# Cross-attention of a perceiver block on one core: values as the stationary operand in the attend, the chunk's sum turned back, and part of the next chunk's keys and values moved in PE's order

## The chip, the cores and the metric

The kernel runs on one core of a Trainium2 chip (the chip has eight). The metric is device time in microseconds of one launch, median of the runs shown. The engines are named as the profile names them: PE (TensorE, with PEld for its weight loads), DVE (VectorE), ACT (ScalarE), POOL (GpSimd), SP (SyncE). PE's clock has two levels, 1.2 and 2.4 GHz; the profile shows the granted clock as a share of the higher one.

## The reference, cut to what matters

Three blocks follow each other on x (8 batches of 128 queries, 512 wide): a cross-attention over a context of 2048 keys (384 wide) with a mask, a self-attention, and a quantised MLP. The change lies in the first.

```python
def _L0_xattn_ref(x, context, mask, W_q, W_k, W_v, W_o, b_o):
    HEADS, DIM_HEAD = 8, 64
    q = (x @ W_q).reshape(b, n, HEADS, DIM_HEAD)
    k = (context @ W_k).reshape(b, j, HEADS, DIM_HEAD)
    v = (context @ W_v).reshape(b, j, HEADS, DIM_HEAD)
    sim = jnp.einsum('bihd,bjhd->bhij', q, k) * DIM_HEAD ** (-0.5)
    sim = jnp.where(mask[:, None, None, :], sim, max_neg)
    attn = jax.nn.softmax(sim, axis=-1)
    out = jnp.einsum('bhij,bjhd->bihd', attn, v).reshape(b, n, INNER)
    return out @ W_o + b_o
x = x + _L0_xattn_ref(_layernorm(x), ctx_768, mask, ...)
x = x + _L0_attn_ref(_layernorm(x), ...)
x = x + _L0_ffn_ref(_layernorm(x), ...)
```

## The kernel before

Everything stays on one core, engine programs are written out by hand and meet through semaphores. The cross-attention walks over batches b and, in each, over chunks of 256 keys (NC = 8 for a batch). A chunk whose keys are all masked is skipped: each engine reads the same bits into a register and branches over it (`live`, lines 260 to 264). With this data 13 of 64 chunks are live, one or two in a batch. The softmax is done with a running maximum: each chunk scales the batch's sum `o_all` by `alpha` and adds its own part.

To keep float32 accuracy, keys and values are products of split operands: `hi` is the rounded part, `lo` the rest, and a product is three terms over three slices of the context (`product`, lines 561 to 572): hi by hi, lo by hi, hi by lo, so nine matmuls.

One live chunk n on PE (`chunk`, lines 659 to 721) works for itself and for the next live chunk, `ahead` = n + 1:

- `scores(g)` (663 to 675) makes the scores of heads 2g and 2g+1, three pairs of matmuls, each with 64 rows of the array, into banks 3 and 4. It waits until DVE has taken the maxima of the pair before.
- `turn_context(ahead)` (623 to 634) transposes the next chunk's context: four transposes into bank 0, two into bank 1.
- `keys(ahead, g)` (636 to 649) makes a quarter of the next keys: nine matmuls of 256 columns; keys 0 and 1 into bank 2, keys 2 and 3 into bank 0.
- `turn(g)` (677 to 688) transposes the probabilities of a pair of heads, four transposes into bank 5 or 6.
- `values(ahead, t)` (651 to 657) makes half of the next values: nine matmuls of 512 columns into bank 1 (t = 0) or bank 2 (t = 1).
- `attend(g)` (690 to 701) multiplies the turned probabilities of a pair (the stationary operand, 128x128) with the values (64 moving columns): two heads by two key tiles, which the trace shows as eight matmuls; the result lies queries by (head, dim) in bank 7.

The order is written out in lines 703 to 721:

```python
scores(0); turn_context(ahead); scores(1); keys(ahead, 0); turn(0)
keys(ahead, 1); scores(2); attend(0); turn(1); keys(ahead, 2)
scores(3); attend(1); turn(2); keys(ahead, 3); values(ahead, 0)
attend(2); turn(3); values(ahead, 1); attend(3)
```

ACT (lines 1044 to 1076) takes the exponentials (`exp(h)`, 1047), copies the turned probabilities of even pairs (`prob_copy`, 1052), rounds the next context (`context_high`, 1030) and the next keys (`key_high`, 1036), and copies the next values (`value_copy`, 1040); it casts the context behind the first two exponentials, and copies the values at the end, when the last attend is done. DVE (lines 1441 to 1487) takes the maximum of a head while it scales and biases its scores (`top(h)`, 1444, into `probs` and `negm`), makes the low parts (`context_low`, 1428, `key_low`, 1436; both run in the helper `low`, line 1342), copies the turned probabilities of odd pairs (1453), rescales `l_all` and `o_all`, and adds bank 7 to `o_all` at the chunk's end (1487, `o_done`).

After the live chunks of a batch PE projects the output of the batch before (`project_output`, line 738) and turns this batch's normalised output and the norm of an earlier one (723 to 736), while all engines step over the masked chunks. SP loads the context of the chunk after next once the transposes of the next have read the buffer (line 325).

The self-attention further down (`attend2`, lines 836 to 847) has the values as the stationary operand, 64 columns wide, and writes two heads to the two halves of the partitions.

Of the kernel before, what the change touches and what calls it, by code (L numbers as in the profile page):

```python
# [14 lines left out]
P = 128  # L15
# [10 lines left out]
def bass_perceiver_block_kernel(nc, x, ctx_768, mask, xa_wq, xa_wk, xa_wv, xa_wo, xa_bo,  # L26
# [29 lines left out]
    with ExitStack() as ctx:  # L56
# [42 lines left out]
        p2_odd1 = sb("p2_odd1", [P, 512])  # L99

# [95 lines left out]
        def sems(engine, names):  # L196
# [10 lines left out]
        (xnT_ps, code_ps, qT_ps, cxT_ps, kT_ps, s_ps, v_ps, pT_ps, pv_ps, onT_ps, lnT_ps, xo_ps, v2_ps, mean_ps, qk_ps,  # L207
         s2_ps, pT2_ps, o2_ps, y2_ps, wT_ps, xqT_ps, g_ps, u_ps, hqT_ps, y_ps) = sems(
            "pe", "xnT_ps code_ps qT_ps cxT_ps kT_ps s_ps v_ps pT_ps pv_ps onT_ps lnT_ps xo_ps v2_ps mean_ps qk_ps "
            "s2_ps pT2_ps o2_ps y2_ps wT_ps xqT_ps g_ps u_ps hqT_ps y_ps")  # L210
        (wq_hi, wk_hi, wo_hi, xnT_hi, qTall_done, qT_hi, cxT_hi, kT_hi, v_done, p_done, alpha_done, pT_act, onT_hi, lnT_hi, xo_done,
         wv2_hi, v2_act, wqk_hi, qT2_done, p2_done, pT2_act, tern_rounded, wo2_hi, oT_hi, wT_act,
         xq_done, xqT_done, sg_done, h_round, hq_done, hqT_done, y_scaled) = sems(
            "act", "wq_hi wk_hi wo_hi xnT_hi qTall_done qT_hi cxT_hi kT_hi v_done p_done alpha_done pT_act onT_hi lnT_hi xo_done "
# [342 lines left out]
        def _(pe):  # L557
# [78 lines left out]
            def keys(n, g):  # L636
                if g == 0:
                    pe.wait_ge(v_done, START + CT * n)
                elif g == 2:
                    pe.wait_ge(cxT_lo, START + 2 * n + 1)  # L640

                def waits(a, b, k):
                    if g == 0 and a == "hi" and k != 1:
                        pe.wait_ge(cxT_lo if b == "lo" else cxT_hi, START + 2 * n + k // 2 + 1)

                last = product(key_bank[g // 2][:, (g % 2) * CHUNK:(g % 2 + 1) * CHUNK],
                               lambda k, w: part(wk, w)[:, k, g * P:(g + 1) * P], lambda k, w: part(cxT, w)[:, k, :], CK, waits)
                if g % 2:
                    last.then_inc(kT_ps, 1)

            def values(n, t):
                if t == 0:
                    pe.wait_ge(cxT_lo, START + 2 * n + 2)
                else:
                    pe.wait_ge(kT_lo, START + 2 * n + 1)
                product(value_bank[t][:], lambda k, w: part(cxT, w)[:, k, t * P:(t + 1) * P],
                        lambda k, w: part(wv, w)[:, k, :], CK).then_inc(v_ps, 1)

            def chunk(b, n):
# [17 lines left out]
                def turn(g):  # L677
                    pe.wait_ge(p_done, START + H * n + 2 * g + 2)
                    if g == 0:
                        pe.wait_ge(onT_lo, START + b)  # L680
                    if g == 1:
# [8 lines left out]
                def attend(g):  # L690
                    if g == 0:
                        pe.wait_ge(v_done, START + CT * n + CT)
                        pe.wait_ge(o_done, START + n)
                    pe.wait_ge(pT_dve if g % 2 else pT_act, START + 2 * n + g // 2 + 1)
                    for j in range(2):
                        h = 2 * g + j
                        for t in range(CT):
                            at = (CT * j + t) * P
# [1127 lines left out]
```

## Time and profile before

| what | value |
|---|---|
| runs shown | 780.3, 784.73, 784.78 us, median 784.73 |
| profiled execution | 780.1 us, span 778.4 us |
| mean granted clock of PE | 0.947 |
| live chunks of the cross-attention | about 68 to 391 us of the span |

The span runs from the first to the last instruction; the execution's own time has a little around it. A row of a timeline has the start and the length in us, engine, line of the kernel, operation, output and inputs by their names, array tile or size, and a count; in brackets what the engine waited for and how long. Rows of one line that follow each other are merged into one, whose length reaches from the first start to the last end. Matmuls overlap, so the next group often starts before the last has ended.

### The profile page before, as it was taken

How to read it: one execution, taken by the hardware profiler on the slowest of the kernel's cores; microseconds unless marked ns; L12 is line 12 of the kernel's file. 1: busy time of each engine (PE TensorE's matmuls, PEld its weight loads, DVE VectorE, ACT ScalarE, POOL GpSimd, SP SyncE). 2: the span in 40 equal slices, each digit the busy share in tenths (PEclk: the TensorE clock that was granted, in tenths of full speed). 3: DMA queues.
4: the chain of work that ended last, by engine and by line, in shares of the span. 5: the costliest groups of instructions: out<-in, count | busy, mean ns of one | idle time of the engine just before them, and what ended most of it. 6: DMA issues, size and time to landing. Idle time of an engine off the chain costs nothing.

```text
span 778.4 us, 14709 instructions
## 1 busy us (share of the span) xinstructions
PE 665.1 (85%) x4244; PEld 519.8 (67%) x4244; DVE 442.5 (57%) x960; ACT 356.1 (46%) x846; POOL 109.7 (14%) x143
## 2 busy tenths in 40 slices
PE   2896597969969696978969989999999899889996
PEld 1675486858858585867858867777777678634553
DVE  6822344444545444554475766666666534699974
ACT  2233233424434233433441136666666534468984
POOL 2581000010010101010020002222222100012211
PEclk9998888988989987998989999999999999999999
DMA  8000000000000000000545774444453243000111
GB/s 311 23 22 22 2 21 21 22 2 22 22 20 22 2 21 22 22 2 20 190 167 193 272 274 163 163 163 163 163 163 136 109 163 118 6 1 15 27 25 42
DMA packets 40064, 64.86 MB, mean 83 GB/s; under 512 B 4056, under 2 KB 20440, under 8 KB 40032
## 3 DMA queue, kind: packets, MB, share of 16 engines
q1 hardware_dynamic: 40032, 64.45, 24.3%
q8 instruction: 18, 0.29, 0.2%
q14 instruction: 14, 0.11, 0.0%
HBM read 53.95 MB, written 10.49 MB: 83 GB/s over the span
## 4 chain that ended last, share of the span: by engine, by line
PE 64%; DVE 13%; issue 11%; DMA 4%; DVEq 3%; ACT 2%; POOL 1%; SPq 0%; ACTq 0%; POOLq 0%
PE bank L570 33%; PE bank L699 6%; PE bank L930 5%; PE bank L687 3%; DMA absw<-in_L_ffn_w_down_dram 3%; PE bank L672 3%; PE bank L938 2%; PE bank L845 2%; PE bank L589 2%; DVE asum L1584 2%; DVE tern L1634 2%; DVE xn_a L1353 1%; PE bank L822 1%; PE bank L880 1%; PE bank L833 1%
## 5 line engine op out<-in xcount | busy, mean ns | idle before, releaser
L1049 ACT ACTIVATE probs<-probs,negm 128x256 f32<-128x256 f32 x104 | 52.1, 501 | 109.0 <-DVE negm L1450 109.0
L1450 DVE CUSTOM_DVE_ANT_0 probs<-bank,bias,negm_old 128x256 f32<-128x256 f32 x104 | 46.0, 480 | 64.2 <-PE bank L672 62.1
L672 PE MATMUL bank<-kT_hi,qT_hi 64*128 64x256 f32 x104 | 23.2, 440 | 51.6 <-issue 47.8
L930 PE MATMUL bank<-w_T,xqT 128*128 128x512 bf16 x256 | 58.4, 379 | 4.6 <-ACT xqT L1231 2.0
L467 POOL TENSOR_TENSOR rstd<-var_eps,neg_half 128x1 f32 (+1 forms) x16 | 10.0, 623 | 329.6 <-DVE var_eps L1513 260.3
L699 PEld LDWEIGHTS bank<-v_sb,pT 128*128 128x128 f32 x416 | 52.3, 191 | 5.5
L699 PE MATMUL bank<-v_sb,pT 128*128 128x64 f32 x416 | 54.7, 274 | 0.0
L1342 DVE TENSOR_TENSOR kT_lo<-bank,kT_hi 128x512 fp32r<-128x512 f32 x28 | 19.4, 692 | 58.2 <-ACT kT_hi L1038 58.2
L672 PEld LDWEIGHTS bank<-kT_hi,qT_hi 64*128 64x128 f32 x104 | 11.3, 214 | 61.3 <-issue 49.9
L1042 ACT COPY v_sb<-bank 128x512 f32<-128x512 f32 x28 | 15.1, 590 | 76.5 <-PE bank L699 73.5
L930 PEld LDWEIGHTS bank<-w_T,xqT 128*128 128x128 bf16 x256 | 24.1, 98 | 34.7 <-issue 2.9
L570 PE MATMUL bank<-cxT_hi,wk_hi 128*128 128x256 f32 x168 | 36.8, 331 | 3.7 <-ACT cxT_hi L1032 3.4
L513 POOL TENSOR_TENSOR p_even<-p_even,rsum 128x512 f32<-128x512 f32 x16 | 18.1, 1129 | 116.0 <-DVE rsum L1613 116.0
L687 PE MATMUL bank<-ident,probs 128*128 128x128 f32 x208 | 32.9, 283 | 0.0
L1584 DVE TENSOR_REDUCE asum<-absw 128x3072 f32 x8 | 26.8, 3351 | 10.3 <-DMA absw<-in_L_ffn_w_down_dram 10.3
L570 PE MATMUL bank<-cxT_lo,wk_hi 128*128 128x256 f32 x168 | 31.1, 295 | 0.3 <-DVE cxT_lo L1342 0.3
L570 PEld LDWEIGHTS bank<-cxT_hi,wk_hi 128*128 128x128 f32 x168 | 26.1, 208 | 7.2 <-ACT cxT_hi L1032 6.4
L570 PE MATMUL bank<-cxT_hi,wk_lo 128*128 128x256 f32 x168 | 30.8, 295 | 0.0
L1603 DVE COPY kT<-bank 128x512 f32<-128x512 f32 x16 | 11.1, 692 | 34.5 <-PE bank L570 34.5
L1152 ACT ACTIVATE p_odd<-bank,nmax 128x128 f32<-128x128 f32 x64 | 22.7, 371 | 15.7 <-DVE nmax L1609 15.7
L1166 ACT ACTIVATE tern_raw<-tern_raw,wscale 128x1024 f32<-128x1024 f32 x24 | 27.0, 1165 | 3.1 <-DVE tern_raw L1628 3.1
L1739 DVE SCALAR_TENSOR_TENSOR h_f<-bank,qs,sg 128x512 f32<-128x512 f32 x32 | 23.9, 747 | 6.3 <-ACT sg L1238 2.9
(236 smaller groups left out, 1691.5 us busy)
## 6 DMA issues: line engine op xcount, KB each, us to landing
tern_dram<-tern SPq DMA_DIRECT2D x8, 768.0 KB, 5.2
tstage<-tern_dram SPq DMA_DIRECT2D x8, 768.0 KB, 4.3
cx<-in_ctx_dram SPq DMA_DIRECT2D x14, 384.0 KB, 2.9
absw<-in_L_ffn_w_gate_dram SPq DMA_DIRECT2D x8, 512.0 KB, 3.7
absw<-in_L_ffn_w_up_dram SPq DMA_DIRECT2D x8, 512.0 KB, 5.3
absw<-in_L_ffn_w_down_dram SPq DMA_DIRECT2D x8, 512.0 KB, 6.8
tern_raw<-in_L_ffn_w_gate_dram SPq DMA_DIRECT2D x8, 512.0 KB, 6.3
tern_raw<-in_L_ffn_w_up_dram SPq DMA_DIRECT2D x8, 512.0 KB, 7.2
```

What stands on the lines that cost most here:

```text
L570: last = mm(to, left(k, a), right(k, b), start=(n == 0), stop=(n == 3 * nk - 1))
L672: last = mm(bank[3 + j][:, 0:CHUNK], part(qT, a)[o:o + DH, g, :], part(kT, c)[o:o + DH, g, :], start=(a == c), stop=(a == "lo"))
L687: last = tr(bank[5 + g % 2][:, at:at + P], probs[:, 2 * g + j, t * P:(t + 1) * P], ident[:])
L699: last = mm(bank[7][:, h * DH:(h + 1) * DH], pT[:, g % 2, at:at + P], v_sb[:, t, h * DH:(h + 1) * DH], start=(t == 0), stop=(t == CT - 1))
L930: last = mm(bank[3 + 2 * which + c % 2][:], xqT[:, u, k * P:(k + 1) * P], w_T[:, which, k, c * 512:c * 512 + 512], start=(k == 0), stop=(k ...
L1049: fn(probs[:, h, :], probs[:, h, :], ACT.Exp, bias=negm[:, h:h + 1], scale=-1.0, accum_out=csum[:, h:h + 1]).then_inc(p_done, 1)
L1152: last = fn(p2[u % 2][j][:, g * P:(g + 1) * P], bank[2 + j][:, g * P:(g + 1) * P], ACT.Exp, bias=nmax2[:, j, g:g + 1], scale=SCALE, accum_ ...
L1166: made = fn(piece, piece, ACT.Copy, bias=ROUND, scale=wscale[:, w:w + 1])
L1342: return tt(to, of, f32(hi), ALU.subtract)
L1450: nc.vector.tensor_tensor_reduce(probs[:, h, :], bank[3 + h % 2][:, 0:CHUNK], bias[:], -SCALE, negm_old[:, h:h + 1], ALU.add, ALU.min, neg ...
L1584: red(asum[:, bass.ds(g, 1), :].rearrange("p a w -> p (a w)"), absw[u][:], AX_X, ALU.add, apply_absolute_value=True).then_inc(absw_done, 1)
L1739: stt(h_f[:, u, c * 512:c * 512 + 512], bank[5 + c % 2][:], qs[:, u, 4:5], sg[:, c % 2, :], ALU.mult, ALU.mult).then_inc(h_done, 1)
```

## The change

The attend has the values as the stationary operand now (64 columns of a head) and the turned probabilities as the moving one (128 columns). The two heads of a pair go to partitions 0 to 63 and 64 to 127 of bank 7, interleaved, so that bank 7 holds the chunk's result turned, dims by queries. ACT copies it to SBUF (into `p2_odd1`, a buffer of a later stage), PE turns it back with four transposes into bank 5, and DVE adds from there. The wait for the sum of the chunk before moves from the first attend to the first turn, since both use bank 5 or 7. The last value product is split: five of its nine matmuls before the last attend, four behind it, ahead of the turn back. The first quarter of the next keys is split as well: the terms hi by hi and lo by hi go before the second scores, hi by lo behind them. ACT rounds the next context before its first exponential.

The hunk left out adds the semaphores `oback_ps` (counted by PE) and `oT_copied` (by ACT) to the lists.

```diff
--- before.py
+++ after.py
@@ -97,6 +97,7 @@
         wscale = sb("wscale", [P, 3])
         qs = sb("qs", [P, 2, 16])
         p2_odd1 = sb("p2_odd1", [P, 512])
+        oT_c = p2_odd1[:].rearrange("p (g q) -> p g q", g=4)
 
         BASE = 25600
         assert nc.sbuf_base <= BASE, nc.sbuf_base
...
@@ -633,28 +634,36 @@
                     last = tr(bank[1][:, t * P:(t + 1) * P], cx[:, t, 2 * P:3 * P], ident[:])
                 last.then_inc(cxT_ps, 1)
 
-            def keys(n, g):
-                if g == 0:
+            KEY_TERMS = (("hi", "hi"), ("lo", "hi"), ("hi", "lo"))
+
+            def keys(n, g, terms=(0, 1, 2)):
+                if g == 0 and 0 in terms:
                     pe.wait_ge(v_done, START + CT * n)
                 elif g == 2:
                     pe.wait_ge(cxT_lo, START + 2 * n + 1)
-
-                def waits(a, b, k):
-                    if g == 0 and a == "hi" and k != 1:
-                        pe.wait_ge(cxT_lo if b == "lo" else cxT_hi, START + 2 * n + k // 2 + 1)
-
-                last = product(key_bank[g // 2][:, (g % 2) * CHUNK:(g % 2 + 1) * CHUNK],
-                               lambda k, w: part(wk, w)[:, k, g * P:(g + 1) * P], lambda k, w: part(cxT, w)[:, k, :], CK, waits)
+                for i in terms:
+                    a, c = KEY_TERMS[i]
+                    for k in range(CK):
+                        if g == 0 and a == "hi" and k != 1:
+                            pe.wait_ge(cxT_lo if c == "lo" else cxT_hi, START + 2 * n + k // 2 + 1)
+                        last = mm(key_bank[g // 2][:, (g % 2) * CHUNK:(g % 2 + 1) * CHUNK], part(wk, a)[:, k, g * P:(g + 1) * P],
+                                  part(cxT, c)[:, k, :], start=(i == 0 and k == 0), stop=(i == 2 and k == CK - 1))
                 if g % 2:
                     last.then_inc(kT_ps, 1)
 
-            def values(n, t):
+            VALUE_TERMS = (("hi", "hi"), ("lo", "hi"), ("hi", "lo"))
+
+            def values(n, t, first=0, end=3 * CK):
                 if t == 0:
                     pe.wait_ge(cxT_lo, START + 2 * n + 2)
-                else:
+                elif first == 0:
                     pe.wait_ge(kT_lo, START + 2 * n + 1)
-                product(value_bank[t][:], lambda k, w: part(cxT, w)[:, k, t * P:(t + 1) * P],
-                        lambda k, w: part(wv, w)[:, k, :], CK).then_inc(v_ps, 1)
+                for i in range(first, end):
+                    (a, c), k = VALUE_TERMS[i // CK], i % CK
+                    last = mm(value_bank[t][:], part(cxT, a)[:, k, t * P:(t + 1) * P], part(wv, c)[:, k, :],
+                              start=(i == 0), stop=(i == 3 * CK - 1))
+                if end == 3 * CK:
+                    last.then_inc(v_ps, 1)
 
             def chunk(b, n):
 
@@ -678,6 +687,7 @@
                     pe.wait_ge(p_done, START + H * n + 2 * g + 2)
                     if g == 0:
                         pe.wait_ge(onT_lo, START + b)
+                        pe.wait_ge(o_done, START + n)
                     if g == 1:
                         pe.wait_ge(lnT_lo, START + b - 2)
                     pe.wait_ge(pT_dve if g % 2 else pT_act, START + 2 * n + g // 2)
@@ -690,20 +700,25 @@
                 def attend(g):
                     if g == 0:
                         pe.wait_ge(v_done, START + CT * n + CT)
-                        pe.wait_ge(o_done, START + n)
                     pe.wait_ge(pT_dve if g % 2 else pT_act, START + 2 * n + g // 2 + 1)
-                    for j in range(2):
-                        h = 2 * g + j
-                        for t in range(CT):
-                            at = (CT * j + t) * P
-                            last = mm(bank[7][:, h * DH:(h + 1) * DH], pT[:, g % 2, at:at + P],
-                                      v_sb[:, t, h * DH:(h + 1) * DH], start=(t == 0), stop=(t == CT - 1))
+                    for t in range(CT):
+                        for j in range(2):
+                            h, o, at = 2 * g + j, DH * j, (CT * j + t) * P
+                            last = mm(bank[7][o:o + DH, g * P:(g + 1) * P], v_sb[:, t, h * DH:(h + 1) * DH],
+                                      pT[:, g % 2, at:at + P], start=(t == 0), stop=(t == CT - 1))
                     last.then_inc(pv_ps, 1)
+
+                def turn_back():
+                    pe.wait_ge(oT_copied, START + n + 1)
+                    for g in range(DK):
+                        last = tr(bank[5][:, g * P:(g + 1) * P], oT_c[:, g, :], ident[:])
+                    last.then_inc(oback_ps, 1)
 
                 scores(0)
                 turn_context(ahead)
+                keys(ahead, 0, (0, 1))
                 scores(1)
-                keys(ahead, 0)
+                keys(ahead, 0, (2,))
                 turn(0)
                 keys(ahead, 1)
                 scores(2)
@@ -717,8 +732,10 @@
                 values(ahead, 0)
                 attend(2)
                 turn(3)
-                values(ahead, 1)
+                values(ahead, 1, 0, 5)
                 attend(3)
+                values(ahead, 1, 5, 9)
+                turn_back()
 
             def turn_output(b):
 
@@ -1056,9 +1073,9 @@
                     cp(pT[:, 0, :], bank[5][:]).then_inc(pT_act, 1)
 
                 act.wait_ge(l_done, START + n)
+                context_high(ahead)
                 exp(0)
                 exp(1)
-                context_high(ahead)
                 exp(2)
                 exp(3)
                 prob_copy(0)
@@ -1072,6 +1089,8 @@
                 prob_copy(2)
                 key_high(ahead, 1)
                 act.wait_ge(pv_ps, START + 4 * n + 4)
+                act.wait_ge(oback_ps, START + n)
+                cp(p2_odd1[:], bank[7][:]).then_inc(oT_copied, 1)
                 value_copy(ahead, 0)
                 value_copy(ahead, 1)
 
@@ -1483,8 +1502,8 @@
                 one(tt(o_b, o_b, heads(alpha[:]), ALU.mult), 2)
                 prob_copy(3)
                 mask_bias(ahead)
-                dve.wait_ge(pv_ps, START + 4 * n + 4)
-                tt(o_b, o_b, bank[7][:].rearrange("p (h d) -> p h d", h=H), ALU.add).then_inc(o_done, 1)
+                dve.wait_ge(oback_ps, START + n + 1)
+                tt(o_b, o_b, bank[5][:].rearrange("p (h d) -> p h d", h=H), ALU.add).then_inc(o_done, 1)
 
             def normalise(b, chunks):
                 dve.wait_ge(l_done, START + chunks)
```

## Rows read from the trace of the kernel before

**Rows 1.** The page, busy time and share of the span, all engines.

```profile
PE 665.1 (85%) x4244; PEld 519.8 (67%) x4244; DVE 442.5 (57%) x960; ACT 356.1 (46%) x846; POOL 109.7 (14%) x143
```

**Rows 2.** View of stages: 13 chunks, us, busy by engine, PEclk, DMA, GB/s.

```profile
...
97.83:116.36 18.53, 18.53 (x133) 16.47 (x133) 8.52 (x28) 7.33 (x23) 0.00 (x0) 0.90 0.06 22
...
173.53:193.55 20.02, 19.94 (x132) 17.75 (x132) 8.52 (x28) 7.44 (x23) 0.00 (x0) 0.84 0.06 20
193.55:212.13 18.58, 17.25 (x133) 15.38 (x133) 9.20 (x29) 8.39 (x25) 0.00 (x0) 1.00 0.07 23
...
sum 248.59, PE 241.57 PEld 215.09 DVE 114.16 ACT 101.11 POOL 0.00; mean PE 18.58 PEld 16.55 DVE 8.78 ACT 7.78 POOL 0.00
```

**Rows 3.** Timeline of PE, start of a second chunk (first scores at 193.55).

```profile
194.10 0.66 PE L629 MATMUL bank<-ident,cx 128*128 128x128 f32 x4
...
195.74 0.39 PE L672 MATMUL bank<-kT_hi,qT_hi 64*128 64x256 f32 x2 [0.76 <-DVE negm L1450]
...
196.92 0.66 PE L570 MATMUL bank<-cxT_hi,wk_hi 128*128 128x256 f32 x3 [0.57 <-ACT cxT_hi L1032]
...
198.20 0.61 PE L687 MATMUL bank<-ident,probs 128*128 128x128 f32 x4
...
199.81 0.39 PE L672 MATMUL bank<-kT_hi,qT_hi 64*128 64x256 f32 x2
```

**Rows 4.** Timelines of ACT and DVE, the same stretch.

```profile
193.66 1.07 ACT L1042 COPY v_sb<-bank 128x512 f32<-128x512 f32 x2 [5.66 <-PE bank L699]
...
196.31 0.56 ACT L1032 CAST cxT_hi<-bank 128x512 fp32r<-128x512 f32 x1
...
195.19 0.48 DVE L1450 CUSTOM_DVE_ANT_0 probs<-bank,bias,negm_old 128x256 f32<-128x256 f32 x1
...
197.84 0.47 DVE L1450 CUSTOM_DVE_ANT_0 probs<-bank,bias,negm_old 128x256 f32<-128x256 f32 x1
```

**Rows 5.** Timeline of PE: attends and the unit behind each.

```profile
200.36 1.10 PE L699 MATMUL bank<-v_sb,pT 128*128 128x64 f32 x8
201.30 0.61 PE L687 MATMUL bank<-ident,probs 128*128 128x128 f32 x4
...
207.99 1.00 PE L699 MATMUL bank<-v_sb,pT 128*128 128x64 f32 x8
208.82 0.61 PE L687 MATMUL bank<-ident,probs 128*128 128x128 f32 x4
...
241.22 1.00 PE L699 MATMUL bank<-v_sb,pT 128*128 128x64 f32 x8
242.15 0.39 PE L672 MATMUL bank<-kT_hi,qT_hi 64*128 64x256 f32 x2
```

**Rows 6.** PE in the second attention: timeline, and line 845's durations (min/median/max).

```profile
506.61 1.07 PE L570 MATMUL bank<-ln_T_lo,wqk_even_hi 128*128 128x512 f32 x4
507.61 1.09 PE L845 MATMUL bank<-pT,v_all 128*64 128x128 f32 x16
508.63 0.39 PE L818 MATMUL bank<-block_mask,onehot 128*128 128x512 bf16 x1
...
L845 PE MATMUL bank<-pT,v_all x256: 272/273/324, 478.8 to 627.3; 128*64 128x128 f32 x128
```

**Rows 7.** Timeline of PE, start of a first chunk (first scores at 173.53).

```profile
174.47 1.11 PE L629 MATMUL bank<-ident,cx 128*128 128x128 f32 x4
...
175.93 0.58 PE L672 MATMUL bank<-kT_hi,qT_hi 64*128 64x256 f32 x2
...
177.02 1.01 PE L570 MATMUL bank<-cxT_hi,wk_hi 128*128 128x256 f32 x3
...
179.11 0.99 PE L687 MATMUL bank<-ident,probs 128*128 128x128 f32 x4
```

**Rows 8.** Timeline of DVE: sixth maximum, copy of the last turned probabilities.

```profile
201.54 0.48 DVE L1450 CUSTOM_DVE_ANT_0 probs<-bank,bias,negm_old 128x256 f32<-128x256 f32 x1
...
209.47 0.69 DVE L1457 COPY pT<-bank 128x512 f32<-128x512 f32 x1 [1.09 <-PE bank L687]
```

More of the change, by code:

```diff
@@ L206, in bass_perceiver_block_kernel @@
         absw_in, tst_in = [absw_in0, absw_in1], [tst_in0, tst_in1]
-        (xnT_ps, code_ps, qT_ps, cxT_ps, kT_ps, s_ps, v_ps, pT_ps, pv_ps, onT_ps, lnT_ps, xo_ps, v2_ps, mean_ps, qk_ps,
+        (xnT_ps, code_ps, qT_ps, cxT_ps, kT_ps, s_ps, v_ps, pT_ps, pv_ps, oback_ps, onT_ps, lnT_ps, xo_ps, v2_ps, mean_ps, qk_ps,
          s2_ps, pT2_ps, o2_ps, y2_ps, wT_ps, xqT_ps, g_ps, u_ps, hqT_ps, y_ps) = sems(
-            "pe", "xnT_ps code_ps qT_ps cxT_ps kT_ps s_ps v_ps pT_ps pv_ps onT_ps lnT_ps xo_ps v2_ps mean_ps qk_ps "
+            "pe", "xnT_ps code_ps qT_ps cxT_ps kT_ps s_ps v_ps pT_ps pv_ps oback_ps onT_ps lnT_ps xo_ps v2_ps mean_ps qk_ps "
             "s2_ps pT2_ps o2_ps y2_ps wT_ps xqT_ps g_ps u_ps hqT_ps y_ps")
-        (wq_hi, wk_hi, wo_hi, xnT_hi, qTall_done, qT_hi, cxT_hi, kT_hi, v_done, p_done, alpha_done, pT_act, onT_hi, lnT_hi, xo_done,
+        (wq_hi, wk_hi, wo_hi, xnT_hi, qTall_done, qT_hi, cxT_hi, kT_hi, v_done, p_done, alpha_done, pT_act, oT_copied, onT_hi, lnT_hi, xo_done,
          wv2_hi, v2_act, wqk_hi, qT2_done, p2_done, pT2_act, tern_rounded, wo2_hi, oT_hi, wT_act,
          xq_done, xqT_done, sg_done, h_round, hq_done, hqT_done, y_scaled) = sems(
-            "act", "wq_hi wk_hi wo_hi xnT_hi qTall_done qT_hi cxT_hi kT_hi v_done p_done alpha_done pT_act onT_hi lnT_hi xo_done "
+            "act", "wq_hi wk_hi wo_hi xnT_hi qTall_done qT_hi cxT_hi kT_hi v_done p_done alpha_done pT_act oT_copied onT_hi lnT_hi xo_done "
             "wv2_hi v2_act wqk_hi qT2_done p2_done pT2_act tern_rounded wo2_hi oT_hi wT_act "
```

## Prediction

> **What bounds the kernel now.** Read the page first: PE is busy for 85% of the span and no other engine for more than 57% [rows 1]. Then the view of stages, cut at the first scores of each of the 13 live key chunks: they last 248.59 us together [rows 2], which is all that the change can touch. Two kinds stand there. Eight chunks are the first of a batch; they come after a pause of PE and begin at the lower of the clock's two levels (the mean granted clock is 0.90 in the shortest, of 18.53 us, and 0.84 in one of the longest, of 20.02). Five are second ones, at 1.00 throughout, all of 18.6 us, so the eight take 19.46 in the mean. In the first kind PE has hardly a gap; in a second one it is busy for 17.25 of 18.58 us [rows 2], so a chunk is bound by PE's own stream of work, save for two waits at its start. Those are seen in PE's timeline of a second chunk [rows 3]. With the first scores (193.55) at 0, PE turns the context (four transposes from 0.55, two more), then waits until 2.19 for the maxima of the first two heads (0.76 idle), and, behind the second scores, until 3.37 for the cast context (0.57 idle); the first turn of probabilities stands at 4.65. The timelines of ACT and DVE say why [rows 4]: ACT spends 1.07 us on the two value copies, takes two exponentials, and only then casts the context, at 2.76, though the transposes that feed the cast end at 1.21 (0.55 + 0.66).
>
> **The change, part by part.** I count from the first matmul of a unit to that of the next, in us, for one chunk.
>
> Attend, before. Eight matmuls with 128x128 stationary take 0.94 to the next unit (200.36 to 201.30), 0.83 behind a value product (207.99 to 208.82), and 0.93 for the last one before scores (241.22 to 242.15) [rows 5].
>
> Attend, after. Stationary is 128x64, moving 128x128, and the two heads of a pair write the two halves of the partitions. That very shape stands in the second attention [rows 6]: 16 matmuls last 1.09, the last one's own length of 0.27 (the median) included, so 15 steps take 0.82, or 0.109 for a pair. From the first to the next unit they take 1.02 (507.61 to 508.63), so leaving costs 0.20 behind the last start. Entering costs too: the last of the four matmuls before it starts at 506.61 + 1.07 - 0.39 = 507.29 (0.39 is what one of 512 columns lasts, as the next unit's row has it) and the first of the shape 0.32 later, where their own step is 0.23: 0.09 more. Eight matmuls then take 0.82 x 7/15 + 0.20 = 0.58. What no row shows is the accumulation over two key tiles in this shape. If the switches cost nothing, it is 8 x 0.0545 = 0.44. If the halves do not run beside each other, each matmul takes the step of a transpose with as many columns, (0.61 - 0.27)/3 = 0.11 [rows 5]: 7 x 0.11 + 0.20 and a slow first step, some 1.03. I take 0.58, the row of the same shape.
>
> The sum for attends: the first two, behind scores, 0.94 to 0.58 each: -0.72. The third, 0.83 to 0.58 + 0.09: -0.16. The fourth with the four transposes that turn the result back: 0.58 + 0.09, and three steps of 0.11 and an exit of 0.20 for the transposes (0.53), is 1.20 in place of 0.93: +0.27. Together **-0.61** in every chunk.
>
> Would the turn back wait? Its input is copied by ACT, 0.54 (half of the two copies' 1.07 [rows 4]). The last attend matmul starts 0.38 behind the first, ends 0.27 later, and the copy is done at about 0.65 + 0.05 + 0.57 + 0.05 = 1.32. PE meanwhile does the four value matmuls that were held back: 0.58 + 4 x 0.23 = 1.50. Hidden, with 0.18 in hand; without that cover PE would stand for some 0.7. Behind the new wait on ACT stand the two value copies, then the cast; they end 0.4 behind the next first scores, and the cast can begin only at 1.25, so nobody waits for them. DVE's sum now waits for the turned result: the last transpose starts 0.2 before the next first scores and ends 0.07 behind them, so the sum starts at 0.13, where what waits for the last attend now starts at 0.11 (193.66 [rows 4]). The maxima and the end of a batch stand as they do. The wait for the sum moves to the first turn, which comes 3 us behind it: free. No DMA moves: SP's context load still waits for the same transposes, which keep their place.
>
> The fourth attend also comes earlier behind the third turn, by the four held-back matmuls. It needs DVE's copy of the turned probabilities, which starts 0.65 behind the turn's first transpose (209.47 against 208.82 [rows 5, 8]) and lasts 0.69: ready about 1.40 behind that transpose. The turn (0.36) and five value matmuls of 0.23 (the first is slow, so I count 1.23) bring the attend to 1.59, with its entry 1.68. In hand 0.28.
>
> The start of a second chunk. The cast is now first on ACT: it starts at 1.25, and keys begin 0.61 behind it (196.31 to 196.92 [rows 3, 4]): 1.86. Two thirds of the nine matmuls' 1.28, and the entry to scores, are done at 2.75; the maxima were ready for scores at 2.19, so the second scores come 0.56 late. They take 0.55 (193.55 to 194.10): 3.30. The last third needs the low half of the context from DVE, two subtractions of 1.02 in all behind the second maximum (which starts at 1.64 and lasts 0.48): from 2.14 to 3.17. PE's last third, 0.43 and 0.10 for the slow first step, ends at 3.83, where the first turn stood at 4.65: **-0.82**. The first two exponentials now end at 3.3, so the turn does not wait.
>
> What is late next? The third maximum, now 0.79 behind the second scores: 3.54 in place of 4.29. In the profile the sixth maximum starts 3.70 behind the third (197.84 to 201.54 [rows 4, 8]), and scores follow a maximum's start by 0.55, so the fourth scores may start at 7.8. PE reaches them behind a turn and nine key matmuls (198.20 to 199.81, 1.61 [rows 3]), scores (0.55), the attend (0.58), and a turn and nine more: 3.83 + 1.61 + 0.55 + 0.58 + 1.61 = 8.18. In hand 0.4; this chain runs closer than before, but does not set.
>
> The start of a first chunk is half at the lower clock [rows 7]. With the first scores at 173.53 [rows 2], the four transposes end at 2.05 (174.47 + 1.11), and keys could begin 0.65 later, at 2.70; now the second scores begin at 2.40, keys at 3.49, and the turn at 5.58. New: six of nine matmuls take 1.39 of 2.09, to 4.15 with the entry; scores 0.94 (173.53 to 174.47), 5.1; the rest 0.70, 5.8. So 0.2 is lost here, since PE waits once for 0.4 instead of twice for 0.1 to 0.2. Where the clock rises elsewhere I bound it by a loss of 0.4 (more of the keys at the lower level) and a gain of 0.3 (the pauses of the second kind in part). I take **+0.1** over the eight.
>
> Sum: second chunks -0.61 - 0.82 = -1.43, five times -7.2; first chunks -0.61 + 0.1 = -0.51, eight times -4.1. Together **-11.2 us**. The profiled execution took 780.1 (span 778.4), so its like would take 768.9. The runs shown have a median of 784.73, 4.6 above it; from that, 773.5. I forecast **773.5**, with 766 to 778 as this case's own range (0.3 us in each of 13 chunks, and the spread of the runs shown). About 1%, 7.8 us, is what a measurement of this kernel can tell from no change.
>
> A rule speaks against the attends. The Trainium skill (TensorEngine Tiling (Array Packing), Tiling Modes) says that "Changing tiling mode (not just tile) drains the TensorE". The second attention shows 0.09 for entering and 0.20 for leaving [rows 6], less than a matmul's length of 0.27 on either side; by a drain of that length the sum would be the first rival's.
>
> **The rivals.**
> *Each switch drains PE in full.* An entry would then cost 0.27 in place of 0.09, and an exit 0.07 more: 0.25 in each of four attends, 1.0 a chunk, 13 in all. 784.73 - 11.2 + 13 = 786.5: no change. Against it: the shape is entered and left for less in the second attention [rows 6]. Chance 0.05. This is the case that the Trainium skill's rule on tiling modes (TensorEngine Tiling (Array Packing), Tiling Modes) would make.
> *The switches cost nothing.* With 0.44 for an attend and no entry, 4 x 0.14 and two entries of 0.09, 0.74 in each chunk, go as well, 9.6 in all: 763.9. For it: accumulating pairs may let weights load ahead; against it: the exit of 0.20 [rows 6]. Chance 0.10.
> *The clock rises later in the first chunks.* Now a first chunk spends twice the missing clock at the lower level: 2 x 0.10 x 18.53 = 3.7 to 2 x 0.16 x 20.02 = 6.4 us [rows 2]. The clock rose after PE had worked on with little pause; the change puts its waits together and the scores, with half of the array's rows, later. If it rises 2.7 us later (the way from the shortest to the longest of these), a chunk loses half of that; in all eight that is 10.8: 784.3, no change; in four, 779. Against it: the sum of PE's waits stays about the same. Chance 0.15.
> *The chain of maxima, exponentials and key casts sets the fourth scores.* It has 0.4 in hand by my reckoning. If it sets, second chunks keep their start as it was, and lose the 0.82: 784.73 - 7.1 = 777.6. Chance 0.07.
> *The halves do not run beside each other* once a pair accumulates. An attend takes 1.03 in place of 0.58, 1.8 more in each chunk, 23.4 in all: 784.73 + 12.2 = 797, slower. It decides where the second of a pair starts 0.054 behind the first: the gain of 11.2 is 0.86 a chunk, over 16 pairs. Against it: the second attention's eight pairs at 0.109 each, which is what one such matmul takes alone [rows 6]. Chance 0.05.
>
> **How the numbers follow.** The forecast has 0.58, the free switches 0.10, the clock 0.15, the chain 0.07, the drain 0.05, the serial halves 0.05. Faster by over 1% (under 776.9): nearly all of the first two, 0.66 in all with a little of the chain's; slower by over 1%: the serial halves, and a little of a clock late in every chunk, 0.06; within 1%: the rest, 0.28. The range runs from 763, just below free switches, to 785, past a clock that rises late in all eight chunks.
>
> **What would show it.** Right: attend groups of eight in 0.58 to the next unit, second chunks of 17.2 us, first turn at 3.8, first chunks about half a microsecond shorter at the same clock, ACT's copy done before the last value matmul starts. Wrong: pairs over 0.06 apart, PE idle before the turned-back transposes, a PE clock under 0.85 in most first chunks, PE idle before the fourth scores, or first chunks that are longer than now.

## The result and the profile after

The changed kernel takes 784.65 us (median of 22 runs, 780.69 to 792.06). The kernel before, run beside it as often, takes 780.99 (777.15 to 784.78), so the three runs shown at first had two from the upper end. The ratio is 1.005, with a 95% interval of 1.0029 to 1.0071: half a percent slower, where 1.4% faster was forecast. The profiled execution took 782.76 us, span 781.0.

The page of the kernel after, answering to [rows 1], and its clock in 40 slices of the span:

```profile
PE 666.7 (85%) x4269; PEld 503.2 (64%) x4296; DVE 442.1 (57%) x960; ACT 363.0 (46%) x859; POOL 109.1 (14%) x143
...
PEclk9998778997979978997998999999999999999999
```

The clock row of the kernel before:

```profile
PEclk9998888988989987998989999999999999999999
```

PE is as busy as before. The clock row has 7s where the cross-attention runs, where it had 8s. The view of stages of the kernel after, in the columns of [rows 2], says which chunks these are:

```profile
97.35:118.89 21.54, 21.15 (x136) 17.15 (x137) 8.70 (x29) 8.99 (x26) 0.00 (x0) 0.78 0.07 20
127.55:147.99 20.44, 19.90 (x137) 16.00 (x137) 8.87 (x29) 8.94 (x26) 0.00 (x0) 0.84 0.07 21
...
176.37:197.85 21.48, 20.95 (x137) 16.96 (x137) 8.84 (x29) 9.05 (x26) 0.00 (x0) 0.79 0.07 20
197.85:215.82 17.97, 17.37 (x136) 13.90 (x137) 9.15 (x30) 8.79 (x26) 0.00 (x0) 1.00 0.07 23
...
307.50:326.91 19.41, 18.83 (x136) 15.08 (x137) 8.89 (x29) 8.83 (x26) 0.00 (x0) 0.89 0.07 22
...
sum 254.59, PE 247.54 PEld 199.13 DVE 116.30 ACT 115.66 POOL 0.00; mean PE 19.04 PEld 15.32 DVE 8.95 ACT 8.90 POOL 0.00
```

The five second chunks did become shorter, 17.8 to 18.0 us in place of 18.6 [rows 2], 3.4 us in all. The eight first chunks became longer: the sum less the second ones leaves 20.63 us each in place of 19.45, 9.4 us in all. Their granted clock is 0.78 to 0.90, where it was 0.83 to 0.91. Reckoned as in the prediction, as twice the missing clock times the length, they spend 7.0 us each at the lower level, where it was 5.3 before. That is not all: at the same clock of 0.84 a first chunk takes 20.44 us (from 127.55) where one took 20.02 [rows 2]. All 13 stages together are 6.0 us longer, the rest of the span 3.4 us shorter, the span 2.6 longer. Of the 3.4, some 2.4 lie in the seven batches' ends, 0.3 in each (10.43 from 165.94 to the next scores at 176.37, where it was 10.77 from 162.76 to 173.53).

PE's timeline of a second chunk of the kernel after, with the end of the chunk before it, answers to [rows 3] and [rows 5]:

```profile
195.33 0.66 PE L707 MATMUL bank<-pT,v_sb 128*64 128x128 f32 x8
195.92 0.50 PE L663 MATMUL bank<-wv_hi,cxT_lo 128*128 128x512 f32 x1
196.26 0.87 PE L663 MATMUL bank<-wv_lo,cxT_hi 128*128 128x512 f32 x3
196.97 0.60 PE L714 MATMUL bank<-ident,p_odd 128*128 128x128 f32 x4
197.85 0.54 PE L681 MATMUL bank<-kT_hi,qT_hi 64*128 64x256 f32 x2 [0.28 <-issue]
...
198.56 0.66 PE L630 MATMUL bank<-ident,cx 128*128 128x128 f32 x4
...
199.89 0.66 PE L649 MATMUL bank<-cxT_hi,wk_hi 128*128 128x256 f32 x3 [0.46 <-ACT cxT_hi L1049]
...
200.84 0.39 PE L681 MATMUL bank<-kT_hi,qT_hi 64*128 64x256 f32 x2
...
201.84 0.60 PE L697 MATMUL bank<-ident,probs 128*128 128x128 f32 x4
```

The attend is as priced: eight matmuls in 0.66, 0.59 to the next unit (195.33 to 195.92). The first turn stands 3.99 behind the first scores (197.85 to 201.84), against 4.65. But the four transposes that turn back take 0.88 to the next scores (196.97 to 197.85) where 0.53 was reckoned, and these scores then take 0.71 (to 198.56) in place of 0.55 [rows 3].

PE's timeline of a first chunk of the kernel after, answering to [rows 7]:

```profile
176.37 0.58 PE L681 MATMUL bank<-kT_hi,qT_hi 64*128 64x256 f32 x2 [5.71 <-issue]
...
178.22 0.63 PE L634 MATMUL bank<-ident,cx 128*128 128x128 f32 x2
179.09 1.01 PE L649 MATMUL bank<-cxT_hi,wk_hi 128*128 128x256 f32 x3 [0.25 <-ACT cxT_hi L1049]
...
182.42 1.06 PE L697 MATMUL bank<-ident,probs 128*128 128x128 f32 x4
```

The context's last transposes start at 178.22, two at 0.225, so PE could go on at about 178.67 (an estimate); the keys start at 179.09, 0.4 later, for ACT's cast. The first turn stands 6.05 behind the first scores, where it was 5.58 [rows 7].

### The profile page after: what moved, and what is told of

The parts are those of the page before. It is cut to its first block, busy times and chain, and to the rows that moved or that the text cites. A ratio compares the mean times of both kernels' runs of the same rounds, so it can differ in the third digit from the quotient of the medians.

```text
span 781.0 us, 14814 instructions
## 1 busy us (share of the span) xinstructions
PE 666.7 (85%) x4269; PEld 503.2 (64%) x4296; DVE 442.1 (57%) x960; ACT 363.0 (46%) x859; POOL 109.1 (14%) x143
## 4 chain that ended last, share of the span: by engine, by line
PE 67%; DVE 13%; issue 11%; DMA 4%; ACT 2%; DVEq 1%; POOL 0%; SPq 0%; ACTq 0%
PE bank L571 17%; PE bank L649 10%; PE bank L663 8%; PE bank L947 5%; PE bank L681 5%; PE bank L697 4%; PE bank L707 4%; DMA absw<-in_L_ffn_w_down_dram 3%; PE bank L955 2%; PE bank L862 2%; PE bank L590 2%; DVE asum L1603 2%; DVE tern L1653 2%; PE bank L630 1%; DVE xn_a L1372 1%
## 5 line engine op out<-in xcount | busy, mean ns | idle before, releaser
L649 PE MATMUL bank<-cxT_hi,wk_hi 128*128 128x256 f32 x168 | 38.6, 344 | 4.8 <-ACT cxT_hi L1049 4.8
L1049 ACT CAST cxT_hi<-bank 128x512 fp32r<-128x512 f32 x14 | 8.2, 585 | 65.1 <-PE bank L630 65.0
L697 PE MATMUL bank<-ident,probs 128*128 128x128 f32 x208 | 35.9, 299 | 0.0
L1093 ACT COPY p_odd<-bank 128x512 f32<-128x512 f32 x13 | 7.6, 586 | 57.2 <-PE bank L707 57.2
L707 PE MATMUL bank<-pT,v_sb 128*64 128x128 f32 x416 | 34.2, 285 | 0.0
L649 PE MATMUL bank<-cxT_lo,wk_hi 128*128 128x256 f32 x168 | 33.7, 313 | 0.5 <-DVE cxT_lo L1361 0.5
L649 PE MATMUL bank<-cxT_hi,wk_lo 128*128 128x256 f32 x168 | 32.5, 307 | 0.0
L707 PEld LDWEIGHTS bank<-pT,v_sb 128*64 128x64 f32 x416 | 21.6, 136 | 12.7 <-issue 4.6
L697 PEld LDWEIGHTS bank<-ident,probs 128*128 128x128 f32 x208 | 24.4, 149 | 6.7 <-issue 6.7
```

The source lines that it names most:

```text
L649: last = mm(key_bank[g // 2][:, (g % 2) * CHUNK:(g % 2 + 1) * CHUNK], part(wk, a)[:, k, g * P:(g + 1) * P], part(cxT, c)[:, k, :], start=( ...
L697: last = tr(bank[5 + g % 2][:, at:at + P], probs[:, 2 * g + j, t * P:(t + 1) * P], ident[:])
L707: last = mm(bank[7][o:o + DH, g * P:(g + 1) * P], v_sb[:, t, h * DH:(h + 1) * DH], pT[:, g % 2, at:at + P], start=(t == 0), stop=(t == CT ...
```

## Experiments

Two theories. A: the new order at the chunk's start (cast, six keys, scores, three keys) leaves PE idle in a first chunk while the clock is low, the clock rises later, and that takes the gain. B: the attends and the turn back do it. Where matmuls are added, they compute something that nobody reads. Each run compares with runs of the kernel before on the same chip. "Lower level" below is twice the missing mean clock times the span, the mean over the runs of a kernel, in us a run; the kernel before has 84.2 (29 runs, mean clock 0.9460), the changed one 98.1 (22 runs, 0.9374).

### One half each

The attends alone: the changed kernel with

```diff
-                keys(ahead, 0, (0, 1))
                 scores(1)
-                keys(ahead, 0, (2,))
+                keys(ahead, 0)
...
-                context_high(ahead)
                 exp(0)
                 exp(1)
+                context_high(ahead)
```

> The change with the old order of keys, scores, cast and exponentials: only the attends with values stationary, the turn back and the split value product. Theory A (the new order at a chunk's start is what lengthens the stretch at the lower clock): the mean granted clock in the first chunks of batches is back at 0.83 to 0.91, as before the change; second chunks take 18.5 to 18.7 us, since the gain of the four attends is eaten by the turn back and the gap behind it; time within 0.5% of the kernel before. Theory B (the attends and the turn back lengthen it): the clock in the first chunks is 0.78 to 0.90 as after the change, and the time is 5 to 9 us over the kernel before.

The order alone: the kernel before with the changed `keys` and the opposite edit.

> The old attends, without a turn back, with the new order of keys, scores, cast and exponentials. Theory A: first chunks at a mean clock of 0.78 to 0.90 and 20.5 us or more in the mean, second chunks about 17.9 us (0.7 less than before the change); time 3 to 8 us over the kernel before. Theory B: first chunks as before the change (19.4 us), second ones 17.9, time 3 to 4 us under the kernel before.

Attends alone: 780.62 us, ratio 0.9998 (0.9978 to 1.0018), lower level 89.3. Order alone: 783.41 (the mean of its runs, 780.65 to 791.57, is 785.56), ratio 1.0062 (1.0027 to 1.0097), lower level 101.5. Stages of the run with the attends alone (a first and a second chunk), then of that with the order alone:

```profile
173.06:193.26 20.20, 19.92 (x137) 16.33 (x137) 8.76 (x29) 9.04 (x26) 0.00 (x0) 0.84 0.06 21
193.26:211.62 18.36, 17.36 (x137) 13.87 (x137) 9.06 (x30) 8.87 (x26) 0.00 (x0) 1.00 0.07 23
```

```profile
127.65:149.29 21.64, 21.39 (x132) 18.90 (x132) 8.69 (x28) 7.45 (x23) 0.00 (x0) 0.78 0.06 19
...
196.94:214.69 17.75, 17.29 (x133) 15.39 (x133) 9.21 (x29) 8.31 (x25) 0.00 (x0) 1.00 0.07 24
```

In the timeline of the second of these runs, the first turn of that second chunk (first scores at 196.94):

```profile
200.77 0.60 PE L689 MATMUL bank<-ident,probs 128*128 128x128 f32 x4
```

Theory A holds in the main: the order alone has the low clock (0.78 in the first chunk shown; its eight lie between 0.78 and 0.90) and the longer time. The attends alone have no longer time, so B as it was stated falls, but they are not free of its cause: with 89.3 they spend 5.1 us more at the lower level than the kernel before (standard error 1.6), a good third of what the whole change adds, and which of their parts does it stays open. The order's gain in second chunks is just what was reckoned, 18.58 to 17.75. The attends gain 0.2 in a second chunk and nothing in all, where 0.61 in each chunk was forecast; in a first chunk at the same 0.84 they lose 0.2 (20.20 for 20.02).

### A shorter pause ahead of a first chunk

Both kernels with 24 matmuls more at a batch's end, where PE steps over masked chunks:

```diff
                 with pe.If(b > 1):
                     turn_norm(b - 2)
+                with pe.If(b < B - 1):
+                    for _ in range(24):
+                        mm(bank[3][:], onehot[:], block_mask[:], start=True, stop=True)
```

> The changed kernel with 24 matmuls more (512 columns, bf16, into bank 3, which the next scores overwrite) at the end of each batch but the last, where PE steps over masked chunks without work, so that PE does not pause before a first chunk. Theory A: the clock stays at its higher level, first chunks take 17.9 to 18.3 us like second ones, and the time falls by about 8 x 2.6 = 21 us against the changed kernel, to some 763. Rival (the first chunks are longer by the work itself and not by the clock): they stay above 20 us and the time does not fall by more than 5 us.

> The kernel before with the same 24 matmuls at the end of each batch but the last. Theory A: first chunks take 18.6 us like second ones, seven of them less by 0.9, time 6 to 7 us under the kernel before; so the changed kernel with busy batch ends is some 8 us faster than this one, which is the change's worth at one clock. Rival as in the other run: no difference to the kernel before.

Changed kernel: 784.66 us, ratio to the kernel before 1.0065 (1.0032 to 1.0099), lower level 47.5. Kernel before (5 runs): 793.12, ratio 1.0155 (1.0128 to 1.0182), lower level 54.4. The expected times were missed. The pause did not go, it became shorter: PE is idle for 2.3 us ahead of the first scores, where it was 5.7. And each of the batches' ends grew by some 1.8 us (12.2 from project to scores, against 10.4), for a reason that no run shows. In the profiled executions only three of the changed kernel's eight first chunks, and one of the kernel before, ran at the higher level throughout; in others the clock fell within 2.5 us of the first scores. What the kernel before lost of its time at the lower level lay in the batches' ends, where PE has little to do (from 25 us to 3), and not in its first chunks (5.3 and 4.9 us each). So neither time tells what it was meant to. Against each other the two differ by 8.5 us, as was expected, but not at one clock. One thing is to be read from the stages of the changed kernel with busy ends:

```profile
178.39:197.83 19.44, 18.70 (x136) 15.06 (x137) 8.84 (x29) 8.93 (x26) 0.00 (x0) 0.91 0.07 22
310.72:328.88 18.16, 17.38 (x137) 13.90 (x137) 8.89 (x29) 8.82 (x26) 0.00 (x0) 1.00 0.08 23
```

Where a first chunk did run at the higher level throughout (1.00), the same instructions take 18.16 us, 0.2 to 0.4 more than a second chunk; at a mean of 0.78 they took 21.5. Most of a first chunk's extra length is the clock's.

### The cast's place, and the place of the keys

The kernel before with only ACT's order changed:

```diff
+                context_high(ahead)
                 exp(0)
                 exp(1)
-                context_high(ahead)
```

> The kernel before with one thing of the change: ACT rounds the next context ahead of its first exponential. Keys stay whole and behind the second scores, so in a first chunk PE can go from the second scores straight into the keys. Theory A1 (the clock rises later because the change takes the second scores away from the place behind the context's transposes and leaves PE idle there): the stretch at the lower clock is as long as before the change or shorter (5.3 us or less for a first chunk); second chunks 17.9 to 18.0 us, first ones 0.1 to 0.4 us shorter; time 4 to 6 us under the kernel before. Rival A2 (the cast's place on ACT, which makes the exponentials late, is what lengthens it): first chunks at a mean clock of 0.78 to 0.90 as in the run with the order alone, time 2 to 5 us over the kernel before.

The same edit on the run with the attends alone:

> The change with its attends, turn back and split value product, and with the cast first on ACT, but with the keys whole and behind the second scores. Theory A1: clock in the first chunks as in the run with the attends alone (5.0 to 5.6 us at the lower level), second chunks about 18.0 us; time 1 to 4 us under the kernel before. Rival A2: 3 to 6 us over it.

Cast first: 773.14 us, ratio 0.9912 (0.9886 to 0.9939), lower level 74.6. With the attends (6 runs): 772.58, ratio 0.9907 (0.9875 to 0.9939), lower level 84.7. Both gained more than was expected: 7.1 us against the kernel before where 4 to 6 was said, and 7.7 where 1 to 4 was. The rival A2 falls: the cast's place does no harm, it is most of what the change has of good. The attends spend more time at the lower level here too, 84.7 for 74.6, and again without a longer time. Stages of the cast first with old attends:

```profile
172.86:192.07 19.21, 19.21 (x132) 17.09 (x133) 8.51 (x28) 7.47 (x23) 0.00 (x0) 0.87 0.07 21
192.07:209.91 17.84, 17.08 (x134) 15.31 (x133) 9.12 (x29) 8.50 (x25) 0.00 (x0) 1.00 0.07 24
```

A second chunk is 17.84, within 0.1 of what the split keys gave, so the split adds little. PE has no idle time in the first chunk (19.21 busy of 19.21): there the second scores stand between the transposes and the keys, and cover the cast.

### Filling the idle time

The order alone, with one matmul more where PE is idle:

```diff
                 turn_context(ahead)
+                pe.wait_ge(v_done, START + CT * ahead)
+                mm(bank[2][:], onehot[:], block_mask[:], start=True, stop=True)
                 keys(ahead, 0, (0, 1))
```

> The order alone (old attends) with one matmul more of 512 columns behind the context's transposes, into the bank that the keys overwrite, where PE is idle for some 0.4 us in a first chunk. Theory A1 in its narrow form (it is the idle time there that the clock answers to): the stretch at the lower clock falls back from 6.5 to about 5.3 us a first chunk and the time to about that of the kernel before or up to 4 us less. If the clock answers instead to what the whole start is made of (the scores, which use half the rows, come later and are followed by three keys only), it stays at 6 us or more and the time at 3 us or more over the kernel before.

774.86 us, ratio 0.9942 (0.9918 to 0.9966), lower level 75.1 in place of 101.5. PE's timeline at the start of a first chunk, then the stages:

```profile
128.18 0.63 PE L633 MATMUL bank<-ident,cx 128*128 128x128 f32 x2
128.60 0.63 PE L708 MATMUL bank<-block_mask,onehot 128*128 128x512 bf16 x1
129.06 1.01 PE L648 MATMUL bank<-cxT_hi,wk_hi 128*128 128x256 f32 x3
```

```profile
126.32:145.64 19.32, 19.32 (x133) 16.94 (x134) 8.61 (x28) 7.23 (x23) 0.00 (x0) 0.89 0.07 21
...
193.47:211.23 17.76, 17.52 (x135) 15.49 (x134) 9.21 (x29) 8.31 (x25) 0.00 (x0) 1.00 0.08 24
```

The added matmul lies where nothing ran, keys start no later (0.88 behind the last transposes' group, as without it), and a first chunk of the same order takes 19.32 at 0.89 where it took 21.64 at 0.78. That pair is one of the widest; the seven first chunks behind the first batch's take 19.33 in the mean with the added matmul and 20.45 without. The narrow form of A holds: it is the idle time there that the clock answers to. The same line was then put into the changed kernel, into the kernel before as a control, and into the two kernels with the cast first (in these three it stands ahead of the second scores, where PE has little idle time to fill):

> The changed kernel with the one matmul behind the context's transposes that fills PE's idle time there. If the clock is what takes the change's gain, the time at the lower level falls from 98 us a run to 85 or less and the time by 6 us or more against the changed kernel, to 774 to 779; second chunks stay at 17.9. If the gap at the chunk's end (sequencer) and the first chunks' own order matter more, it stays within 3 us of the changed kernel.

> The kernel before with the same matmul behind the context's transposes; PE waits there only some 0.1 us in a first chunk, so this is the control. Expected: no more than 4 us less time at the lower level (84 us a run without it), first chunks 0 to 0.2 us longer at one clock, time within 3 us of the kernel before.

> The attends of the change, the cast first on ACT, keys whole behind the second scores, and the filling matmul. Without it such a kernel took 85 us at the lower level and 772.6. If it is idle time in the first chunks' start that the clock answers to, 75 to 80 us and a time of 766 to 770, the fastest of all; if not, 772 to 775.

> The kernel before with the cast first on ACT and the filling matmul, old attends. Without it 74.6 us at the lower level and 773.1. Expected 70 to 75 us and 771 to 774: the start has little idle time left to fill.

| kernel with the filling matmul | us | ratio to before (95%) | lower level, without | with |
|---|---|---|---|---|
| changed | 775.28 | 0.9927 (0.9898 to 0.9956) | 98.1 | 74.6 |
| before | 778.99 | 0.9981 (0.9959 to 1.0002) | 84.2 | 82.2 |
| attends, cast first | 773.41 | 0.9915 (0.9883 to 0.9948) | 84.7 | 76.5 |
| cast first | 775.43 | 0.9932 (0.9904 to 0.9961) | 74.6 | 75.1 |

Stages of the changed kernel with the filling matmul:

```profile
174.21:193.85 19.64, 19.07 (x136) 15.39 (x138) 8.89 (x29) 8.83 (x26) 0.00 (x0) 0.89 0.07 22
193.85:211.66 17.81, 17.21 (x136) 13.81 (x138) 9.11 (x30) 8.79 (x26) 0.00 (x0) 1.00 0.08 24
```

One matmul whose result is overwritten makes the changed kernel 9.4 us faster (784.65 to 775.28; the kernel before, on the two chips, 780.99 and 780.10) and turns its loss of 0.5% into a gain of 0.7%; in the kernel before, which had little idle time there, it does nothing that can be told. So the matmul as such does not raise the clock earlier, the filled gap does. With attends and cast first it took 8 us from the lower level and nothing from the time. In the one profiled execution of each, the first chunks are as they were (5.4 us each at the lower level for 5.6, 19.7 us long for 19.6), and the batches' ends, where PE has little to do, have 17 us for 25. That fits, but at six runs each it is not shown.

### The gap at a chunk's end

> The changed kernel with the turn back ahead of the four value matmuls that follow the last attend. Theory S (PE's sequencer stands at the wait for ACT's copy, and only then works through the end of the loop and the head of the next chunk, about 1.1 us, with 0.4 of PE's work left): PE is idle for about 0.7 us ahead of the turn back, but the time from the last of the chunk's matmuls to the next scores falls to 0.25 or less, and the scores take 0.55 in place of 0.71. Rival T (the gap is a switch from float32 transposes to the half-array scores): the four value matmuls behind the transposes start 0.4 or more behind the last transpose, and scores after values take 0.55 as they did.

```diff
-                values(ahead, 1, 5, 9)
                 turn_back()
+                values(ahead, 1, 5, 9)
```

PE's timeline at the end of a chunk:

```profile
147.62 0.66 PE L707 MATMUL bank<-pT,v_sb 128*64 128x128 f32 x8
148.96 0.66 PE L714 MATMUL bank<-ident,p_odd 128*128 128x128 f32 x4 [0.69 <-ACT p_odd L1093]
149.37 0.48 PE L663 MATMUL bank<-wv_hi,cxT_lo 128*128 128x512 f32 x1
149.68 0.86 PE L663 MATMUL bank<-wv_lo,cxT_hi 128*128 128x512 f32 x3
150.48 0.39 PE L681 MATMUL bank<-kT_hi,qT_hi 64*128 64x256 f32 x2
...
151.03 0.44 PE L630 MATMUL bank<-ident,cx 128*128 128x128 f32 x2
```

PE idles 0.69 ahead of the turn back, as theory S expected. The rival T falls: a unit of four transposes is left after 0.41 (148.96 to 149.37). The next scores start without idle time, 0.80 behind the group of three values (150.48 against 149.68; two steps of 0.23 are the group's own, so 0.34 behind the last of them, where S had 0.25 or less), and take 0.55 again (to 151.03). Branches and register operations stand in the trace under PE's sequencer (its queue is PEldq). Where it stands is told by the row of its count of live chunks, which is the first register operation once a chunk's last matmul is queued. The row has the line (760 before, 777 after), the queue, the count, the length in ns, and the first and last start. Of the kernel before and of the changed one:

```profile
L760 PEldq ALU_OP  x13: 32/32/32, 86.1 to 388.5; - x13
```

```profile
L777 PEldq ALU_OP  x13: 32/32/32, 86.8 to 393.0; - x13
```

Before, it ran at 388.5 for the last chunk, 1.1 us ahead of the last attend's start (389.57 in the same trace); after, at 393.0, 0.3 ahead of the turn back (393.28). Both distances are the same in all 13 chunks. The sequencer used to be a microsecond ahead of the array, and now stands at the wait for ACT's copy until just before the transposes, with the loop's end, a branch and the next scores' waits still to do: in the changed kernel the next scores start 1.2 us behind this operation (197.85 against 196.7), with PE idle for 0.28. The kernel with the turn back first was run once, 789.98 us at a mean clock of 0.934. Both lie within the changed kernel's own range (780.69 to 792.06, 0.928 to 0.946), so that run tells nothing of the order's worth.

## Why the prediction was wrong

The forecast was -11.2 us, and the profiled span is 2.6 longer. Second chunks gave -3.4 for -7.2, first chunks +9.4 for -4.1, and the rest of the span -3.4 where nothing was forecast ("the end of a batch stand as they do": it is 0.3 shorter). So the steps that failed are the term of the first chunks, by the clock and by their own work, and the turn back in the sum of the attends.

*The attend, 0.58.* Right: 0.59. The second attention's row priced it, accumulation over two key tiles costs nothing, and the two rivals of a full drain and of halves that don't run beside each other fall. The Trainium skill's rule that a change of tiling mode drains PE (TensorEngine Tiling (Array Packing), Tiling Modes) does not show as a full drain: eight matmuls with their exit take 0.59 where the row's prices gave 0.58, and where a drain of a matmul's length on either side would add 0.25 by the prediction's own reckoning.

*The turn back, 0.53, "Hidden, with 0.18 in hand".* This term was mis-sized. ACT's copy was hidden as reckoned (196.04 to 196.63, transposes at 196.97), but the wait also holds PE's sequencer, which no step had counted: 0.88 to the next scores for 0.53, and 0.16 more in these scores. The four values behind the attend took 1.05 for 0.92, and a turn behind an attend 0.41 for 0.37. For a second chunk before scores the parts are: two attends and turns 2 x (1.00 - 1.31) = -0.62; the third with the value product -0.11; the last with values and turn back 1.32 + 0.59 + 1.05 + 0.88 = 3.84 for 2.14 + 0.93 = 3.07, +0.77; scores +0.16. Together +0.20 in place of -0.61. With the attends alone a second chunk is still 0.22 shorter, since its late first scores cost less than they seem to: PE then waits 0.28 us for the maxima where it waited 0.76 [rows 3]. Over the run the attends won nothing (0.9998).

*The start of a second chunk, -0.82.* Right: with the order alone the first turn stands at 3.83 (200.77 less 196.94) and the chunk takes 17.75 for 18.58. Most of it is the cast's: with the cast first and whole keys the chunk takes 17.84.

*The start of a first chunk, +0.1.* Too small: where it lay at the lower level it is +0.47 (6.05 for 5.58). With the attends, which lose in a first chunk too, a first chunk is 0.4 longer at the same clock (20.44 for 20.02), where it was to be 0.51 shorter. That is about half of the miss in the first chunks, and would be there without any change of the clock.

*The clock.* The third rival came in part. It was priced at 10.8 us if the clock rises 2.7 us later in all first chunks, and put aside with a chance of 0.15 and the argument that "the sum of PE's waits stays about the same". The sum does, 0.4 for 0.1 to 0.2 twice. What that argument missed is that one gap of 0.4 us in the first work counts: filled, it gives the time back. Over all runs the changed kernel spends 13.9 us more at the lower level. In the stages a first chunk of one kernel is some 0.4 to 0.55 us longer for each us more at that level (20.02 for 18.53 us at 6.4 and 3.7 us [rows 2] is 0.55, 21.54 for 19.41 at 9.5 and 4.3 here is 0.41), so some 6 to 7.5 us are lost by it, an estimate. The mean time rose by 3.9 (781.02 to 784.94), so all the rest of the change gained 2 to 4 us, not 11.2. The fill shows the cause, not only the coincidence: without the gap the loss goes. But even then the kernel gains 0.7%, half of what was forecast, since the two terms above stay. How much of the 13.9 is the attends' (5.1 when they stand alone) is open.

*From 768.9 to 773.5.* The median of three runs was 3.7 us above that of 22. The scatter of this kernel, 777 to 786, is in good part the clock's: over 29 runs the time and the time at the lower level have a correlation of 0.75, and over the changed kernel's 22 runs 0.94. Two numbers of the prediction come near the measured 784.65 by luck: the upper end of its wider range, 785, and the 784.3 of the clock's rival. Both stand on the high base, and the rival also keeps the full gain of the other terms.

## What to carry to other kernels

Where PE's clock is low at the start of a stretch, a short wait there can cost more than its length (here 0.4 us in each of eight chunks, and 9.4 us came back when it was filled): look at what PE does without a pause until its clock is up, and keep a unit that needs nothing new (here the second scores) in front of one that waits. A wait that PE meets last in a loop's body must be priced with the loop's own overhead, since here the sequencer did not run ahead of it (0.3 us ahead, where it had been 1.1). Compare what belongs together at one clock before the clock is blamed for all: here the first chunks had become longer at the same clock too. Of this change the cast's earlier place on ACT gives by itself as much as any variant that was run, 0.9%, with no new work on any engine.

## What was not expected of the hardware

One matmul of 512 columns, in a gap of 0.4 us in each first chunk, took the time at the lower clock from 98.1 to 74.6 us a run. With 2.3 us of idle time ahead of a first chunk the clock was still at its higher level at the first scores, and in some chunks fell within the next 2.5 us. Matmuls put behind a batch's end, where PE only steps over branches, were not free: 24 of them made that stretch 1.8 us longer (12.2 for 10.4).
